# An eleven-layer decoder on one core: expert routing moved into the attention stream before it, and the Hadamard layer's order of work set for each engine

## What is computed

```python
# level 1, feed-forward ("Hadamard layer"); quantised = round, clip to -128..127
inter = silu(quant8(x) @ ternary(w_gate).T) * (quant8(x) @ ternary(w_up).T)   # 512 -> 2048
y     = quant8(fwht(inter)) @ ternary(w_down).T                               # 2048 -> 512
# level 2, attention and cross-attention: 16 heads of 32, causal softmax, fp32
# level 2, feed-forward: 64 experts, 8 per token, hidden width 192
scores = softmax(x @ gate_weight.T); w, idx = top_k(scores, 8); w = w / sum(w)
y = sum over the 8 experts e of w_e * (silu(x @ w_gate[e]) * (x @ w_up[e])) @ w_down[e]
```

## Time and profile before

| | |
|---|---|
| median of three runs | 5755.03 us |
| the profiled execution's own time | 5776.2 us |
| its span | 5774.9 us |
| busy share of the span | PE 79%, DVE 58%, ACT 27%, POOL 32% |
| `l1_ffn` | about 2389 to 2776 us of the span |
| `l2_attn` | about 2785 to 3750 us |
| routing, to the first expert product | 3750 to 3994 us |
| expert blocks and final sums | to 4960 us |

### The profile page before, as it was taken

One profiled execution on the slowest core, in us unless ns is written; L12 is line 12 of the kernel. 1 busy time (PEld: TensorE's weight loads), 2 busy tenths in 40 slices (PEclk: granted clock), 3 DMA queues, 4 the chain that ended last, 5 costly groups with the idle time before them and its releaser, 6 DMA issues. The chain is left out here.

```text
span 5774.9 us, 65500 instructions
## 1 busy us (share of the span) xinstructions
PE 4554.2 (79%) x23078; PEld 2456.4 (43%) x23078; DVE 3328.7 (58%) x5551; ACT 1540.4 (27%) x2961; POOL 1846.3 (32%) x1793
## 2 busy tenths in 40 slices
PE   7996888999955642588799889723999998597687
PEld 5772222444433532355333333321555554243376
DVE  5866776677659985799445565450333332455522
ACT  1114666211111100444122223200121211254332
POOL 1233221001136666244101111145555554111411
PEclk9997999999965555788899999856999999798698
DMA  4320000100000002100001110023999997101000
GB/s 142 97 60 8 2 1 2 70 0 0 0 10 0 0 0 29 67 1 1 30 27 39 49 36 16 6 92 78 229 243 234 222 217 145 62 1 41 2 1 30
DMA packets 156356, 330.86 MB, mean 57 GB/s; under 512 B 25713, under 2 KB 39666, under 8 KB 154483
## 3 DMA queue, kind: packets, MB, share of 16 engines
q1 hardware_dynamic: 109154, 226.37, 12.6%
q0 software_dynamic: 46880, 100.30, 8.9%
HBM read 376.93 MB, written 78.45 MB: 79 GB/s over the span
## 5 line engine op out<-in xcount | busy, mean ns | idle before, releaser
L204 PE MATMUL ps<-arena 128*128 128x512 f32 (+17 forms) x18762 | 3987.2, 451 | 599.9 <-DMA arena<-in_L_gamma 83.2
L204 PEld LDWEIGHTS ps<-arena 128*128 128x128 f32 (+7 forms) x18762 | 1913.7, 167 | 2470.2 <-issue 1344.7
L209 PE MATMUL ps<-arena 128*128 128x128 f32 (+2 forms) x3292 | 441.5, 277 | 568.6 <-DMA arena<-moe_x,arena 154.3
L209 PEld LDWEIGHTS ps<-arena 128*128 128x128 f32 (+2 forms) x3292 | 363.2, 143 | 746.7 <-issue 453.5
L254 POOL TENSOR_SCALAR arena<-arena 128x1 f32<-128x1 f32 x192 | 73.6, 384 | 1168.6 <-DVE arena L248 1168.4
L2650 DVE SCALAR_TENSOR_TENSOR arena<-ps,arena 128x128 f32<-128x128 f32 x382 | 103.6, 313 | 541.0 <-ACT arena L2534 477.8
L2709 POOL DMA_INDIRECT moe_y<-arena x191 | 306.7, 1606 | 299.6 <-DVE arena L2667 232.2
L2097 DVE TENSOR_REDUCE arena<-ps 128x2 f32<-128x256 f32 (+3 forms) x256 | 199.2, 821 | 291.3 <-PE ps L204 291.3
L865 DVE TENSOR_REDUCE arena<-ps 128x2 f32<-128x1024 f32 x256 | 304.0, 1219 | 83.3 <-PE ps L204 82.5
L2135 POOL TENSOR_SCALAR_AFFINE_SELECT arena<-arena 128x512 f32<-128x512 f32 x128 | 81.6, 638 | 749.5 <-ACT arena L2073 749.5
L2073 ACT ACTIVATE arena<-ps 128x1024 f32<-128x1024 f32 (+3 forms) x256 | 166.2, 701 | 545.9 <-PE ps L204 545.9
(11 more groups left out here) (295 smaller groups left out, 4246.4 us busy)
## 6 DMA issues: line engine op xcount, KB each, us to landing
arena<-in_L_ffn_gu SPq DMA_DIRECT2D x191, 768.0 KB
arena<-in_L_ffn_dn SPq DMA_DIRECT2D x191, 256.0 KB
arena<-in_L_ffn_dn SPq DMA_DIRECT2D x191, 128.0 KB
arena<-in_L_ffn_w SPq DMA_DIRECT2D x64, 256.0 KB
arena<-in_L_ffn_w_gate SPq DMA_DIRECT2D x32, 256.0 KB
arena<-in_L_ffn_w_up SPq DMA_DIRECT2D x32, 256.0 KB
arena<-in_L_ffn_w_down SPq DMA_DIRECT2D x32, 256.0 KB
moe_y<-arena SPq DMA_DIRECT2D x8, 1024.0 KB
```

The lines of the kernel that those rows point to most:

```text
L204: return self.nc.tensor.matmul(out, lhsT, rhs, start=start, stop=stop, skip_group_check=True)
L209: return self.nc.tensor.transpose(out, in_, ident[0:n, 0:n])
```

## The change

**Hadamard layer.** `skew` is replaced by an order for each engine. TensorE: hadamard, down, up, turn. ScalarE: hadamard, scale, down, half of up, clip, the other half, turn, quant. VectorE: quant, stats, hadamard, clip, down, up. GpSimd: hadamard, down. Of the three 2048-wide passes VectorE keeps one ("clip": max and min at once); ScalarE scales and adds the constant before it ("scale") and subtracts the constant behind it ("clip", into bf16). The last 512-wide pass also goes to ScalarE ("quant").

**Routing.** It moves into the last 46 ticks of `l2_attn`, tile by tile. For an output tile n of the cross-attention at tick t: normalise at t+1, transpose at t+2, logits and store to DRAM at t+3, exponential and choice at t+4, rank at t+5, 8 scatters at t+6, two per tick over four ticks (for the last four tiles all eight at t+6). The rank of a tile needs only the counts of the tiles before it, as each expert now has 2048 places of its own (`c_route` holds the first place of each; the table in DRAM has 1025 rows of 128 places). A list of blocks follows the last rank ("table"). The table is fetched at the start of `l2_ffn` by two indirect DMAs that take one row of 128 places for each block, then turned by four transposes on TensorE and two copies on VectorE. `y0` starts as the tokens and not as zeros, so the final sum needs one addition fewer. The zeros of `y1` and the empty table are written during `l1_ffn`. `norm_x` of an attention output now has a place of its own, one tick after the output.

Ahead of a route step's first write of its places VectorE waits for all scatters of the tile two before; each scatter waits for the same-numbered one of the tile before.

```diff
-    LAGS = (0, 1, 2, 3, 4, 5)
+    LAG = dict(quant=0, turn=1, up=2, up2=2, hadamard=3, stats=4, scale=4, clip=4, down=5)
+    def order(names):
+        for t in range(NT + 5):
+            for what in names.split():
+                if 0 <= t - LAG[what] < NT:
+                    yield what, t - LAG[what]
...
+        for what, i in order("hadamard down up turn"):
...
+        for what, i in order("hadamard scale down up clip up2 turn quant"):
...
+            elif what == "scale":
+                act.wait_ge(dve, "hscale", i)
+                act.wait_ge(pool, "magic")
+                nc.scalar.activation(HA[i % 2], HA[i % 2], ACT.Identity, bias=MG[:, 0:1], scale=m[:, 5:6]).then_inc(
+                    *act.done("rounded", i))
+            elif what == "clip":
+                act.wait_ge(dve, "clip", i)
+                act.wait_ge(pe, "yt", i - 2, 1) if i >= 2 else None
+                nc.scalar.activation(YB[i % 2], HA[i % 2], ACT.Identity, bias=MG[:, 1:2]).then_inc(*act.done("yb", i))
+            elif what == "quant":
+                act.wait_ge(dve, "xq", i)
+                act.wait_ge(pe, "xt", i - 2)
+                act.wait_ge(pool, "magic")
+                nc.scalar.activation(XB[i % 2], XQ[i % 2], ACT.Identity, bias=MG[:, 1:2]).then_inc(*act.done("xb", i))
...
-        for s, i in skew(NT, LAGS):
+        for what, i in order("quant stats hadamard clip down up"):
...
-                nc.vector.tensor_scalar(XQ[i % 2], XQ[i % 2], -128.0, MAGIC, ALU.max, ALU.add).then_inc(*dve.done())
-                dve.settle()
-                dve.wait_ge(pe, "xt", i - 2)
-                nc.vector.tensor_scalar(XB[i % 2], XQ[i % 2], MAGIC, None, ALU.subtract).then_inc(*dve.done("xb", i))
-            elif s == 2:
+                nc.vector.tensor_scalar(XQ[i % 2], XQ[i % 2], -128.0, MAGIC, ALU.max, ALU.add).then_inc(*dve.done("xq", i))
...
-                nc.vector.tensor_scalar(ha, ha, m[:, 5:6], 127.0, ALU.mult, ALU.min).then_inc(*dve.done())
-                dve.settle()
-                nc.vector.tensor_scalar(ha, ha, -128.0, MAGIC, ALU.max, ALU.add).then_inc(*dve.done())
-                dve.settle()
-                dve.wait_ge(pe, "yt", i - 2, 1) if i >= 2 else None
-                nc.vector.tensor_scalar(YB[i % 2], ha, MAGIC, None, ALU.subtract).then_inc(*dve.done("yb", i))
-            elif s == 5:
+            elif what == "clip":
+                ha = HA[i % 2]
+                dve.wait_ge(act, "rounded", i)
+                nc.vector.tensor_scalar(ha, ha, MAGIC - 128.0, MAGIC + 127.0, ALU.max, ALU.min).then_inc(*dve.done("clip", i))
...
+        dma.start(sp, k.mTW.rearrange("(p a) c -> p (a c)", p=P), ins["c_slots"], "slots")
+        sp.wait_ge(pool, "zero")
...
+def route_pe(k, what, i, ring):
+    pe, act, dve, dma = k.pe, k.act, k.dve, k.dma
+    if what == "route":
+        pe.wait_ge(dve, "x", NT + i)
+        b = quad(ring.take("lt", i, by=((act, "lt", i),)))
+        for kk in range(4):
+            t = k.tr(b[:, kk, :], k.X[:, i, kk * P:kk * P + P])
+        t.then_inc(*pe.done("lt", i))
+    elif what == "logits":
+        r = ring.take("logits", i, by=((dve, "logits", i),))
+        pe.wait_ge(act, "lt", i)
+        pe.wait_ge(dma, "route w")
+        for kk in range(4):
+            t = k.mm(r[:, 0:NE], k.rLX[i % 2][:, kk, :], k.rWR[:, kk, :], kk == 0, kk == 3)
+        t.then_inc(*pe.done("logits", i))
+    elif what == "rank":
+        r = ring.take("rank", i, by=((dve, "slot", i),))
+        pe.wait_ge(dma, "route c")
+        pe.wait_ge(dve, "chosen", i)
+        pe.wait_ge(dve, "cum", i - 1)
+        t = k.mm(r[:, 0:NE], k.rTRI[:, 0, :], k.rMM[i % 2], True, i == 0)
+        if i:
+            t = k.mm(r[:, 0:NE], k.rTRI[:, 1, :], k.rCU[i % 2], False, True)
+        t.then_inc(*pe.done("rank", i))
...
+def route_act(k, what, i, ring):
+    nc, pe, act, dve = k.nc, k.pe, k.act, k.dve
+    if what == "route":
+        act.wait_ge(pe, "lt", i)
+        act.wait_ge(pe, "logits", i - 2)
+        nc.scalar.activation(k.rLX[i % 2], quad(ring.of("lt", i)), ACT.Copy).then_inc(*act.done("lt", i))
+    elif what == "exp":
+        act.wait_ge(dve, "shift", i)
+        nc.scalar.activation(k.rEE[i % 2], k.rEE[i % 2], ACT.Exp, bias=k.rT8[i % 2][:, 0:1], accum_out=k.rT8[i % 2][:, 1:2]).then_inc(
+            *act.done("exp", i))
...
+def route_dve(k, what, i, ring):
+    nc, pe, act, dve, pool, dma = k.nc, k.pe, k.act, k.dve, k.pool, k.dma
+    j = i % 2
+    ee, mm, rw, sc, t8, s8 = k.rEE[j], k.rMM[j], k.rRW[j], k.rSC[j], k.rT8[j], k.rS8[j]
+    if what == "logits":
+        dve.wait_ge(pe, "logits", i)
+        nc.vector.tensor_copy(ee, ring.of("logits", i)[:, 0:NE]).then_inc(*dve.done("logits", i))
+        dve.wait_ge(dve, "logits", i)
+        nc.vector.tensor_reduce(t8[:, 0:1], ee, AX.X, ALU.max, negate=True).then_inc(*dve.done("shift", i))
+    elif what == "exp":
+        dve.wait_ge(act, "exp", i)
...
+        nc.vector.tensor_tensor(mm, k.rREST, ee, ALU.not_equal).then_inc(*dve.done("chosen", i))
...
+    elif what == "rank":
+        b8, pay = k.rB8[j], k.rPAY[j]
+        dve.wait_ge(pe, "rank", i)
+        nc.vector.tensor_tensor(sc, ring.of("rank", i)[:, 0:NE], k.rFIRST, ALU.add).then_inc(*dve.done("slot", i))
...
+        for s in k.slot_in if i >= 2 else ():
+            dve.queue.wait_ge(s, 16 * (i - 1))
+        nc.vector.tensor_scalar(k.rIX[j].bitcast(U32), s8, -1.0, None, ALU.add).then_inc(*dve.done("at", i))
+        nc.vector.tensor_copy(pay[:, :, 0], k.rTOK[:, i:i + 1].to_broadcast([P, 8])).then_inc(*dve.done("token", i))
...
+        nc.vector.tensor_reduce(pay[:, :, 1], b8, AX.X, ALU.add).then_inc(*dve.done("w8", i))
...
+def route_pool(k, i, n):
+    dve, pool, dma = k.dve, k.pool, k.dma
+    pool.wait_ge(dma, "slots", stage="l1ffn")
+    pool.wait_ge(dve, "at", i)
+    pool.wait_ge(dve, "w8", i)
+    pool.queue.wait_ge(k.slot_in[n], 16 * i) if i else None
+    k.nc.gpsimd.indirect_dma_start(k.mTW, bass.IndirectOffsetOnAxis(ap=k.rIX[i % 2][:, n:n + 1].bitcast(U32), axis=0),
+                                   k.rPAY[i % 2][:, n, :], None).then_inc(k.slot_in[n], 16)
...
+    over = {16 * b + 32 + ((6, 7, 14, 15) if b < 7 else (3, 4, 5, 6))[j]: 4 * b + j for b in range(8) for j in range(4)}
+    late = {103: [("routes", 0)]}
+    for t, n in over.items():
+        late.setdefault(t + 1, []).append(("x", n))
+        if n >= NT:
+            for lag, what in ((2, "route"), (3, "logits"), (4, "exp"), (5, "rank")):
+                late.setdefault(t + lag, []).append((what, n - NT))
+            for j in range(8):
+                late.setdefault(t + 6 + (j // 2 if n < 28 else 0), []).append(("scatter", 8 * (n - NT) + j))
+            late.setdefault(t + 3, []).append(("store", n - NT))
...
+            for what, n in late.get(t, ()):
+                yield what, n
+                if (what, n) == ("rank", NT - 1):
+                    yield "table", 0
...
+            elif what == "store":
+                xv, yv = (a.rearrange("(t p) d -> p t d", p=P) for a in (k.mXD, k.mYD[0]))
+                sp.wait_ge(dve, "x", NT + n)
+                dma.start(sp, xv[:, n, :], k.X[:, n, :], "xd", n)
+                dma.start(sp, yv[:, n, :], k.X[:, n, :], "y0", n)
+            elif what == "table":
+                sp.wait_ge(dve, "experts")
+                dma.start(sp, k.mEB.rearrange("(p j) -> p j", p=P), k.mex.rearrange("p j c -> p (j c)").bitcast(I32), "eb")
...
-                k.norm(n, LAST)
+                k.norm_stats(n)
+            elif what == "x":
+                k.norm_x(n)
...
+        r = R.take("table", by=((dve, "table"),))
+        for j in range(2):
+            pe.queue.wait_ge(table_in[j], 16)
+            for c in range(2):
+                t = k.tr(r[:, 256 * c + P * j:256 * c + P * j + P], GB[:, j, :].rearrange("p (n c) -> p c n", c=2)[:, c, :])
...
-            nc.vector.tensor_tensor(y0[:, i % 4, :], y0[:, i % 4, :], y1[:, i % 4, :], ALU.add).then_inc(*dve.done("y01", i))
-            dve.wait_ge(dve, "y01", i)
             dve.wait_ge(dve, "x", i - 4)
-            nc.vector.tensor_tensor(k.zb[i % 4], k.X[:, i, :], y0[:, i % 4, :], ALU.add).then_inc(*dve.done("z", i))
...
+        for slot in k.slot_in:
+            pool.queue.wait_ge(slot, 16 * NT)
+        for j in range(2):
+            nc.gpsimd.indirect_dma_start(GB[:, j, :], None, TW.rearrange("(r n) c -> r (n c)", n=P),
+                                         bass.IndirectOffsetOnAxis(ap=k.mrow[:, j:j + 1].bitcast(U32), axis=0)).then_inc(table_in[j], 16)
...
+    sl = np.zeros((1025 * P, 2), f)
+    sl[:, 0] = 2048 + np.arange(1025 * P) % P
+    d["c_slots"] = sl.reshape(P, 2050)
```

417 lines of the change are left out of this document (180 added, 237 removed).

## The result

The changed kernel takes 5605.85 us (median of three runs, 5603.02 to 5610.99) against 5755.03; the ratio is 0.974, 95% interval 0.972 to 0.977. The forecast was 5594 us with a range of 5540 to 5645, so the time lies inside it, 12 us above the forecast. The profiled execution took 5610.99 us with a span of 5609.8. Between the two profiled executions the gain is 165 us, where the sum said 161; between the medians it is 149, since the profiled execution of before lay 21 us above its median and this one only 5. The total is nearly right by luck: two terms were wrong by 25 us each, in opposite directions.

The account below looks back on a forecast made before the run. VectorE was taken to bound the Hadamard layer, TensorE level 2's attention, and no engine was full over the routing. Terms −171 − 11 − 11 + 32 = −161 from 5755 gave 5594 us, range 5540 to 5645.

Parts of the forecast that it names:

- (a): Front of the experts, up to the first expert product: GpSimd's scatters become the chain; −171 us, bounds −160 and −177.
- (b): Final sum: one of two additions goes; −11 us, bound −5.
- (c): Hadamard layer: VectorE no longer the bound, period 22.8 us instead of 23.5; −11 us, bounds −47 and +8.
- The ring: Hadamard layer: waits between TensorE and ScalarE set the period, 17.15 us plus the down product.
- So nothing raises the clock, and I take 22.8: Hadamard layer: down product stays below full clock at 5.6 us, giving a period of 22.8 us.
- the two idles: Hadamard layer: TensorE idle about 2.7 and 0.7 us ahead of the down product, so its clock isn't raised.
- rival A: Hadamard layer: shorter idles bring full clock, down product 3.45 us, period 20.6, layer −47, total 5558 us; chance 0.20.
- (d): Attention stream: routing twelve tiles adds 25 us on TensorE, 12 on VectorE, less 5; +32 us, bounds +10 and +70.
- rival B: Attention stream stalls on VectorE, every routing step counts: +70 us instead of +32, total 5632 us; chance 0.19.
- The sign for rival B: Attention stream: masks over 7.5 us apart would show the stall on VectorE.
- rival C: Attention stream: scatter landings of 10.5 us hold each of the last 43 ticks, +176 us, total 5770 us; chance 0.02.
- rival D: Front of the experts: scatter descriptors wait for VectorE, 0.69 us each over 42, losing 29 us, total 5623; chance 0.03.

Follow-up runs that it names:

- Experiment 1: The changed kernel with the Hadamard layer as it was before (order, passes, butterflies on GpSimd), routing and final sum still changed: 5638.5 us, ratio 0.979.
- experiment 2: The changed kernel with ScalarE's copies of the transposed result (down) ahead of the 2048-wide scale pass in the Hadamard layer: 5582.0 us, ratio 0.969.
- experiment 3: The changed kernel with the Hadamard layer's moved passes kept but each engine in the old order, oldest tile first: 5833.2 us, ratio 1.013.
- experiment 4: The changed kernel with TensorE waiting for ScalarE's scale pass ahead of the transposes of down, not behind them: 5625.7 us, ratio 0.977.
- Experiments 6: The changed kernel with the 128x512 comparison in placing done four times instead of once on VectorE for the first twelve tiles: 5635.4 us, ratio 0.979.
- experiment 7: The changed kernel with the logits of the first twelve tiles computed three times over on TensorE: 5605.3 us, ratio 0.974.
- experiment 8: The changed kernel with VectorE's placing cut from the rank step and put a tick later for the first twelve tiles, scatters too: 5584.7 us, ratio 0.970.

## Why the prediction was right in sum, and where its steps failed

**(a) held: −172 for −171.** The chain on GpSimd was as worked out, 42 scatters behind the last norm at 1.29 us with what lies between. The landing took 5.2 us instead of 1, the two fetches with their issues 10.9 (3834.86 to 3845.76) instead of 9.8. Against that the wait for weights, of which 6.6 us were to stay, went wholly, and GpSimd's scatters held the last norm by 1.7 us instead of 3. VectorE's last ranks weren't done near 3796 but near 3816, behind its waits for landings; the scatters covered that. The block loop took 5.5 us less, for which the sum had no term: 3.1 of them are waits for weights that are gone, the rest is open.

**(b) held: −11.9 for −11.** Where loads from DRAM would be late next, they weren't.

**(c) failed in one number: −36 for −11.** The ring was right: 20.50 less 3.45 us of down product leaves 17.05, forecast 17.15. The failed step is "So nothing raises the clock, and I take 22.8". In most periods the clock stayed at 1.00 through the down product, though TensorE still waited 2.69 us. Of the two idles that the prediction put ahead of that product only this one stood there: the transposes followed the Hadamard products with no wait, and the other, 0.62 us, stood ahead of the Hadamard transposes. This was rival A, with a chance of 0.20: its period of 20.6 came in all but a few tiles, and its −47 was missed by those and by the layer's first and last tiles. Experiment 1 puts the part at 33 us by itself, experiment 2 shows that the ring was the bound, and experiment 3 that its order is what made the gain. What exactly decides between the two clocks stays open: experiment 4 had both in one layer with the same waits. That VectorE's passes would come free of GpSimd's butterflies was wrong too: L265 takes their place, at 2.5 us in 11 of 16 tiles. No wait of TensorE shows a cost of it: the two in a period are 2.69 us for ScalarE and 0.62 for VectorE.

**(d) failed in its mechanism: +57 for +32.** The sum took 25 us from TensorE's products, 12 from VectorE and gave 5 back. Experiments 6 and 7 show the reverse: TensorE's work is nearly free there, VectorE's costs about its own length. 12 tiles × 5.7 us, put at 70, was rival B's figure, and the stream came nearer to that (+57) than to the forecast. The failing step is the comparison of 5.2 us of routing in a tick with 3.2 us of idle time "to spare in a tick": that was 78.0 us over 24 waits, not over the ticks. In the last 39 ticks it was 58.9 us, or 1.5 in a tick. The 12 us for such meetings were at least the 21 that experiment 8 took back, and the sum had no term for the clock: 0.87 in place of 0.96, 14.4 us of the same products' time. The clock was higher again where TensorE idled less (0.93 and 0.94 in experiments 7 and 8, with 33 and 34 us of idle against 43), but no run changes the idle time alone. The sign for rival B, masks over 7.5 us apart, didn't show, since it was set against the mean tick of 6.42 us: they lay 6.62 us apart, 1.42 more than the same ticks before.

**Rivals C and D.** GpSimd waited 5.0 us in all for landings within the stream (five times), far from rival C's 4 us a tick. From issue to landing a scatter took 4.9 us in the median and 9.1 at the longest, so single landings are longer than a tick, but the order left them time. Against rival D, the scatters:

```profile
L2055 POOL DMA_INDIRECT moe_slots<-arena x128: 954/961/1804, 3510.6 to 3828.7; - x128
```

Their median is 961 ns and their mean 993, with VectorE busy beside many of them; before, they were 962 and 989. The Trainium skill, page "SBUF — State Buffer", section "SBUF: two separate sides", describes an exclusive lock between VectorE and GpSimd. The trace agrees for arithmetic passes (the 524 ns of such a pass are 2.5 us beside butterflies) and shows none for the scatters, by this median; whether any of VectorE's passes beside them was of the kind that holds the lock, no run here shows.

## To carry to other kernels

When passes are moved between engines, write out the ring of waits that the new order makes, and price it before the engines' sums: the same moved passes gave −33 us with one set of orders and +195 with another (experiments 1 and 3). When work is put into a stream of another engine's, ask not only how much that engine idles, but in which ticks; two steps that meet in one tick cost what a step alone would have hidden. Take the length of a tick from the ticks that the work goes to, not from the mean. And work for TensorE that falls into its own waits can be free: here 18 us more of it left the time the same (experiment 7).

## What was not expected of the hardware

- 175 products more in the same stretch raised TensorE's busy time by 7.0 us (215.3 to 222.3), with the granted clock up from 0.87 to 0.93 (experiment 7).
- With nearly the same waits around the same transposes (2.67, then 0.67 or 0.90 us), TensorE ran 47 products in 12.2 us in one period and in 10.3 in another (experiment 4).
- Behind the last scatter its landing is waited for about 5 us (5.24 us in the changed kernel, 4.3 to 6.1 in the eleven others where the wait is named after it), and the next scatter still issues 1.26 us after the one before.
- The product of gate and up, which reads PSUM and SBUF, isn't lengthened beside GpSimd's butterflies: L1733 took 745 ns on average in this layer, L1700 744 before, while L265, over SBUF alone, took 2.5 us in 11 of 16 tiles, both of them inside the 10.4 us in which GpSimd works at the butterflies.
